# The gate stage of a forgetting attention inside the ramp of its unit loop, and the place of one bit step

## What is computed

```python
q = x @ Wq; k = short_conv(x @ Wk, kconv_w); v = short_conv(x @ Wv, vconv_w)   # 4 taps, silu
q = group_rmsnorm(q, qnw, H); k = group_rmsnorm(k, knw, H)
log_fgate = jax.nn.log_sigmoid(x @ Wf + bf)
cum = jnp.transpose(jnp.cumsum(log_fgate, axis=1), (0, 2, 1))
scores = jnp.einsum('bhtd,bhsd->bhts', qh, kh) * scale + cum[:, :, :, None] - cum[:, :, None, :]
attn = jax.nn.softmax(jnp.where(causal, scores, -jnp.inf), axis=-1)
out = jnp.einsum('bhts,bhsd->bhtd', attn, vh)
out = out / rms(out) * onw * silu(x @ Wg); x = x + out @ Wo
```

## Time and profile before

| | |
|---|---|
| median of 3 runs | 2194.36 us (2193.86 to 2197.66) |
| the profiled execution | 2199.9 us, its span 2198.1 us |
| mean granted TensorE clock | 0.939 |
| PE busy | 1852.4 us (84%) |
| DVE busy | 1541.4 us (70%) |
| ACT busy | 1384.8 us (63%) |
| POOL busy | 1008.2 us (46%) |
| DMA | 84.48 MB, mean 38 GB/s |

### The profile page before, as it was taken

The page is one execution under the profiler, slowest core; times in us unless marked ns, Lnnn a source line. Parts: engine busy times, 40 slices in busy tenths (PEclk is TensorE's granted clock), DMA queues, the critical chain, the costliest instruction groups (busy, mean ns, idle before and its releaser), DMA issues. The chain is left out here.

```text
span 2198.1 us, 36564 instructions
## 1 busy us (share of the span) xinstructions
PE 1852.4 (84%) x12003; PEld 892.8 (41%) x12003; DVE 1541.4 (70%) x2303; ACT 1384.8 (63%) x2346; POOL 1008.2 (46%) x1088
## 2 busy tenths in 40 slices
PE   5558886686976757999999999999999877799996
PEld 2123332542664412555555555555554323222222
DVE  5979996696356957888888888888887637511212
ACT  3547773443344435777777777777776434799995
POOL 0157773363115604676666666666666512400001
PEclk9779998798997978999999999999999979999999
DMA  3000000000000011121211212222122101412110
GB/s 95 0 15 0 0 0 0 1 1 1 0 0 1 1 56 35 48 63 59 61 61 61 60 59 59 59 60 61 61 61 61 41 10 38 120 45 54 49 44 39
DMA packets 71432, 84.48 MB, mean 38 GB/s; under 512 B 20544, under 2 KB 44032, under 8 KB 71168
## 3 DMA queue, kind: packets, MB, share of 16 engines
q1 hardware_dynamic: 69536, 81.69, 12.8%
q10 hardware_dynamic: 1728, 0.67, 0.1%
HBM read 71.95 MB, written 9.57 MB: 37 GB/s over the span
## 5 line engine op out<-in xcount | busy, mean ns | idle before, releaser
L1744 DVE SCALAR_TENSOR_TENSOR fu_kv<-fu_ps_kv,fa_vec,fu_kv 128x511 f32<-128x511 f32 (+2 forms) x384 | 286.3, 746 | 58.9 <-ACT fu_kv L1616 53.7
L2149 ACT ACTIVATE rt_p<-rt_ps_s 128x1024 f32<-128x1024 f32 x256 | 240.3, 1040 | 23.0 <-PE rt_ps_o L2094 17.7
L1827 POOL TENSOR_TENSOR fu_ds<-fu_p 128x768 f32<-128x768 f32 x64 | 115.8, 1809 | 187.8 <-PE fu_ps_ss L1515 185.1
L1475 PE MATMUL fu_ps_s<-fu_qn,fu_kn 64*128 64x512 f32 (+3 forms) x1024 | 190.0, 468 | 1.3 <-ACT fu_p L1675 0.8
L624 POOL TENSOR_TENSOR scan_hC<-scan_h,scan_c 128x1024 f32<-128x1024 f32 x64 | 151.0, 2359 | 71.6 <-DVE scan_h L600 71.6
L1616 ACT ACTIVATE fu_kv<-fu_ps_kv,fa_vec 128x512 f32<-128x512 f32 x128 | 88.3, 690 | 110.6 <-PE fu_ps_kv L1524 67.8
L1505 PE MATMUL fu_ps_n<-fu_p,fu_vt 128*64 128x512 f32 (+3 forms) x1024 | 151.9, 439 | 0.0
L523 PE MATMUL scan_ps_y<-scan_hC,w_ident 128*128 128x512 f32 x256 | 125.7, 614 | 26.4 <-POOL scan_hC L624 14.8
L600 DVE TENSOR_TENSOR_SCAN scan_h<-scan_dA,scan_ps_b 128x1024 f32<-128x1024 f32 x64 | 146.4, 2287 | 2.2
L2094 PE MATMUL rt_ps_o<-rt_p,rt_va 128*32 128x512 f32 x1024 | 137.8, 610 | 10.6 <-ACT rt_p L2149 8.1
L1843 POOL TENSOR_TENSOR fu_kn<-fu_ks,fu_rb 128x512 f32<-128x512 f32 x64 | 81.5, 1273 | 73.4 <-DMA fu_rb<-rms_rows 73.4
(11 more groups left out here) (373 smaller groups left out, 5110.9 us busy)
## 6 DMA issues: line engine op xcount, KB each, us to landing
fu_rb<-rms_rows SPq DMA_DIRECT2D x256, 128.0 KB, 2.9
fu_ro<-rms_rows SPq DMA_DIRECT2D x128, 128.0 KB, 3.0
ra_stackq<-rope_parts SPq DMA_DIRECT2D x168, 32.0 KB
ra_stackk<-rope_parts SPq DMA_DIRECT2D x168, 32.0 KB
w_X<-in_xT SPq DMA_DIRECT2D x4, 512.0 KB, 7.3
fa_wp<-in_wp SPq DMA_DIRECT2D x8, 256.0 KB
fa_cr<-ncum_rows SPq DMA_DIRECT2D x128, 3.0 KB
rope_parts<-ra_hi SPq DMA_DIRECT2D x16, 128.0 KB, 2.7
```

The costliest lines, as they stand in the source:

```text
L1475: pe.matmul(sps[:, h, at:at + T - t * P], k[head(h), t * P:(t + 1) * P], q[head(h), t * P:T], start=(at == 0), stop=False)
L1744: dve.scalar_tensor_tensor(acc, kvps[:, at, 0:T - j], vec[:, a % GA, w:w + 1], acc, ALU.mult, ALU.add).then_inc(done, 1)
L1827: pool.tensor_tensor(DS[:, :, :], P0[p % 2][:, :, P:T], P13[:, :, 0:3 * P], ALU.add).then_inc(s.d1, 1)
L2149: act.activation(pr[k % 2][i][:, :, :], sps[(U * n + u) % RING][:, :, :], ACT.Exp, scale=DH_B ** -0.5).then_inc(s.exp, 1)
```

## The change

The stage forget_gates is removed. Its weight loads go to SP and its memsets to GpSimd in the layernorm "ln5", which now runs inside the function of the attention. Its computation goes into forget_units: the 8 matmuls behind those of unit 1 (into the PSUM tile nps), Abs, Exp and Ln on ScalarE in front of unit 2's tanh, the minimum and the first subtraction on VectorE behind unit 2's keys, the scan with the first split behind unit 3's keys and the rest of the split behind unit 4's. SP stores `ncum_rows` in slot i = -3, loads the broadcasts RB in front of the gate rows CR, and waits for the store before the first CR. ScalarE loads the table of exp and tanh at the start of the block. Scratch is taken from NUM tiles that are not in use yet, and three new tiles. The bit step moves from the end of the odd slot to the next, even slot, behind the cast and the subtraction of the maxima and in front of the taps. Renamed loop variables of TensorE are left out of the diff.

```diff
-def layernorm_stage(nc, name, w, src, dst, loading=False):
+def layernorm_stage(nc, name, w, src, dst, loading=False, held=None):
...
+            if held is not None:
+                @block.sync
+                def _(sp):
+                    sp.dma_start(held.vec[:, :, :], w.vecg_dram.rearrange("g p c -> p g c")).then_inc(held.loaded, 16)
+                    for g in range(GA):
+                        sp.dma_start(held.wp[:, g, :, :], w.wp_dram[g]).then_inc(held.loaded, 16)
+                    sp.dma_start(held.wo[:, :, :], w.woa_dram.rearrange("g p c -> p g c")).then_inc(held.loaded, 16)
+                    sp.wait_ge(held.loaded, 16 * (GA + 2))
+                @block.gpsimd
+                def _(pool):
+                    for k in range(3):
+                        pool.memset(held.cr[k][:, :], 0.0).then_inc(s.zero, 1)
+                    pool.memset(held.mhl[:, :, :, :], 0.0).then_inc(s.zero, 1)
+                    pool.wait_ge(s.zero, 4)
+                    for h in range(2):
+                        for k in range(3):
+                            pool.memset(held.cr[k][64 * h:64 * h + 5, :], 1.0).then_inc(s.made, 1)
+                    pool.wait_ge(s.made, 6)
+                    pool.memset(held.mhl[:, :, :, 0:3], 1.0).then_inc(s.made, 1)
...
-        forget_gates(nc, w, XN, ncum_rows, held)
+        layernorm_stage(nc, "ln5", w, X, XN, held=held)
         forget_units(nc, w, X, XN, ncum_rows, held)
...
# SP of forget_units
-                sp.wait_ge(held.loaded, 16 * (GA + 2))
-                sp.wait_ge(held.stored, 16)
                 for i in range(-AHEAD, U + OUT + 2):
+                    if i == 5 - AHEAD:
+                        sp.wait_ge(s.hi1, 1)
+                        sp.wait_ge(s.mid, 1)
+                        sp.wait_ge(s.lo, 1)
+                        sp.dma_start(ncum_rows, NC[:, :, :]).then_inc(held.stored, 16)
                     u = i + 2
                     if real(u):
                         n, g = divmod(u, GA)
-                        sp.wait_ge(s.sc, seen(u - 2, 3))
-                        for h in range(2):
-                            row = HEADS_A * n + 2 * g + h
-                            sp.dma_start(CR[u % 3][64 * h:64 * h + KF, :], ncum_rows[row, :, :]).then_inc(crs[u % 3], 16)
                         sp.wait_ge(s.put, 16 * (u // WIN + 1))
...
                                 sp.dma_start(RB[head(h), j, :], roots_dram[u // WIN, row:row + 1, :].broadcast_to([64, T])).then_inc(s.rb, 16)
+                        if u == 0:
+                            sp.wait_ge(held.stored, 16)
+                        sp.wait_ge(s.sc, seen(u - 2, 3))
+                        for h in range(2):
+                            row = HEADS_A * n + 2 * g + h
+                            sp.dma_start(CR[u % 3][64 * h:64 * h + KF, :], ncum_rows[row, :, :]).then_inc(crs[u % 3], 16)
...
# TensorE, behind maximum(m, ((0, 0), (2, P)))
+                    if d == 0:
+                        for odd in range(2):
+                            for q in range(B // 2):
+                                f = pe.matmul(nps[32 * q:32 * q + 32, :], w.wf[:, odd, :], XN[:, 2 * q + odd, :], start=(odd == 0), stop=(odd == 1))
+                        f.then_inc(s.f, 1)
...
# ScalarE
+                act.preload_act_table_set("exp_and_others")
                 act.wait_ge(held.loaded, 16 * (GA + 2))
...
+                    if a == 2:
+                        act.wait_ge(s.f, 1)
+                        act.activation(ab[:, :], nps[:, :], ACT.Abs, bias=w.vecs[:, 3:4]).then_inc(s.ab, 1)
+                        act.wait_ge(s.ab, 1)
+                        act.activation(e1[:, :], ab[:, :], ACT.Exp, scale=-1.0).then_inc(s.e, 1)
+                        act.wait_ge(s.e, 1)
+                        act.activation(ln1[:, :], e1[:, :], ACT.Ln, bias=w.one[:, 0:1]).then_inc(s.ln, 1)
                     if real(a):
                         tanh(a, place(a), s.k3, s.thk)
...
# VectorE
                         dve.tensor_tensor(MHL[:, :, :, 4], nm[:, :, :], MHL[:, :, :, 3], ALU.subtract).then_inc(s.ml, 1)
+                    if i % WIN == 0 and windows(i - 2) != (None, None):
+                        begin(i - 1)
                     if real(a):
                         tap(a, 1, 0, place(a), s.tapk, s.k1)
...
                     if real(o):
                         output(o)
+                    if a == 2:
+                        dve.wait_ge(s.ab, 1)
+                        dve.tensor_scalar(mn[:, :], nps[:, :], w.vecs[:, 3:4], 0.0, ALU.add, ALU.min).then_inc(s.mn, 1)
+                        dve.wait_ge(s.mn, 1)
+                        dve.wait_ge(s.ln, 1)
+                        dve.tensor_tensor(ng[:, :], ln1[:, :], mn[:, :], ALU.subtract).then_inc(s.ng, 1)
+                    if a == 3:
+                        dve.wait_ge(s.ng, 1)
+                        dve.wait_ge(s.set, 5)
+                        dve.tensor_tensor_scan(cum[:, :], ones[:, :], ng[:, :], 0.0, ALU.mult, ALU.add).then_inc(s.cum, 1)
+                        dve.wait_ge(s.cum, 1)
+                        dve.tensor_copy(NC[:, 0, :], cum[:, :]).then_inc(s.hi1, 1)
+                        dve.wait_ge(s.hi1, 1)
+                        dve.tensor_tensor(r1[:, :], cum[:, :], NC[:, 0, :], ALU.subtract).then_inc(s.l1, 1)
+                    if a == 4:
+                        dve.wait_ge(s.l1, 1)
+                        dve.tensor_copy(NC[:, 1, :], r1[:, :]).then_inc(s.mid, 1)
+                        dve.wait_ge(s.mid, 1)
+                        dve.tensor_tensor(r2[:, :], r1[:, :], NC[:, 1, :], ALU.subtract).then_inc(s.l2, 1)
+                        dve.wait_ge(s.l2, 1)
+                        dve.tensor_copy(NC[:, 2, :], r2[:, :]).then_inc(s.lo, 1)
...
-                    if q is not None or v is not None:
-                        begin(i)
...
# GpSimd
                 pool.wait_ge(held.loaded, 16 * (GA + 2))
+                pool.memset(ones[:, :], 1.0).then_inc(s.set, 1)
```

More of the change, by code:

```diff
@@ L145, in layernorm_stage @@
         lnv, rstd, step1, step2, fine = ([st.sb(f"{n}{k}", [P, T]) for k in range(2)] for n in ("lnv", "rstd", "v1", "v2", "fine"))
-        s = st.sems("cent kept sq var lnv rstd vr vrr fine wide norm")
+        s = st.sems("cent kept sq var lnv rstd vr vrr fine wide norm zero made")
         with st.block() as block:
@@ L1362, in forget_units @@
         nm = st.sb("nm", [P, NT, 2])
+        ab, e1, ln1, mn, ng, cum = NUM[0:6]
+        r1, r2, ones = (st.sb(n, [P, T]) for n in ("low1", "low2", "ones"))
+        NC = held.nc
         SG = st.sb("sg", [P, T])
@@ L1369, in forget_units @@
         nps, ssps = st.ps("n", [P, T]), st.ps("ss", [P, T])
-        s = st.sems("set kp vp tapk tapv k1 k2 k3 v1 v2 v3 thk thv sk sv vt vc qp qc q2 kk sa so dsq msq mso fold bits ya yb yc yd y1 ye yf yg yh yi r rb ro0 ro1 put "
+        s = st.sems("f ab e ln mn ng cum hi1 l1 mid l2 lo set kp vp tapk tapv k1 k2 k3 v1 v2 v3 thk thv sk sv vt vc qp qc q2 kk sa so dsq msq mso fold bits ya yb yc yd y1 ye yf yg yh yi r rb ro0 ro1 put "
                     "cr0 cr1 cr2 qn kn qm km mx red hi ml rt rr sc ex pv d1 d2 ds n2 nc gp tg sg gated og wo x")
@@ L1536, in _ @@
                         pe.wait_ge(s.ml, b + 1)
-                        for t in range(NT):
-                            k = pe.transpose(mps[:, 1, :].bitcast(BF16)[:, t * P:(t + 1) * P], MHL[:, t, :, :].rearrange("p h c -> p (h c)"), w.identb[:, :])
+                        for j in range(NT):
+                            k = pe.transpose(mps[:, 1, :].bitcast(BF16)[:, j * P:(j + 1) * P], MHL[:, j, :, :].rearrange("p h c -> p (h c)"), w.identb[:, :])
                         k.then_inc(s.rt, 1)
@@ L1550, in _ @@
                         pe.matmul(kvps[:, 1, :], wp[:, g, 2, :], XN[:, n, :], start=True, stop=True).then_inc(s.vp, 1)
-                    if real(f):
-                        pe.wait_ge(s.sv, f + 1)
-                        pe.wait_ge(s.vc, f)
+                    if real(t):
+                        pe.wait_ge(s.sv, t + 1)
+                        pe.wait_ge(s.vc, t)
                         pe.wait_ge(s.nc, seen(p))
-                        for t in range(NT):
-                            k = pe.transpose(nps[:, t * P:(t + 1) * P], VS[f % 2][:, t * P:(t + 1) * P], w.ident[:, :])
+                        for j in range(NT):
+                            k = pe.transpose(nps[:, j * P:(j + 1) * P], VS[t % 2][:, j * P:(j + 1) * P], w.ident[:, :])
                         k.then_inc(s.vt, 1)
@@ L1573, in _ @@
                     if real(p):
-                        pe.wait_ge(s.vc, seen(f + 1))
+                        pe.wait_ge(s.vc, seen(t + 1))
                         pe.wait_ge(s.ex, 3 * p + 3)
@@ L2232, in hybrid_kernel @@
             lambda: None, lambda: ffn0_stages(nc, w, X),
-            lambda: layernorm_stage(nc, "ln5", w, X, XN), lambda: forgetting_attention_stages(nc, w, X, XN),
+            lambda: None, lambda: forgetting_attention_stages(nc, w, X, XN),
```

66 lines of the change are left out of this document (3 added, 63 removed).

## The result

The changed kernel takes 2205.43 us, median of 19 executions (2202.23 to 2211.89); the kernel before took 2199.08 us, median of 19 in the same comparison (2193.86 to 2205.51). The ratio is **1.0028, with a 95% interval of 1.0017 to 1.0038**: slower by 3.7 to 8.4 us. Single executions of one kernel lie up to 12 us apart here, so the traces are compared by stretches. The two profiled executions (2202.23 us, and 2199.9 before) already differ when the changed part begins: the layernorm's first matmul starts at 781.03 us instead of 784.47. They differ again behind it: from the last addition to the end it is 428.0 instead of 430.8 us. What the change does stands between these two points.

The account below looks back on a forecast made before the run. TensorE bounds the unit loop, so other engines matter only through waits holding it up. Terms: -6.3 (gates moved) + 0 + 16.5 - 3.0 - 0.7 = +6.5 us on 2194.36, or 2201 us; own range 2197 to 2206, overall 2186 to 2206.

Parts of the forecast that it names:

- Steady loop: Even slots i = 6 to 54: bit step held by GpSimd's third sum, taps 0.66 us later, 25 times, +16.5 us.
- The precedent of the earlier trace: Late slots before the change: a bit step took 1.49 us instead of 0.19, ending where GpSimd's sum ends.
- Start of the loop: Gate stage in front of the unit loop removed, weight loads hidden under the layernorm: loop starts 12.4 us sooner.
- Ramp: Gate work returning among the first units: slot 2 +3.6 us, slots 3 and 4 +4.1, together +7.7.
- Absorbed at the fold: Ramp, before unit 6's taps: waits for the late fold and a projection shrink, hiding part of the delay, -1.6 us.
- Load order: SP's queue, root broadcasts before gate rows: no effect as TensorE is the bound, 0, between -1 and +1 us.
- End of the loop: Slots 58, 60 and 62: TensorE's wait for the subtraction goes, 3 x 1.0 = -3.0 us.
- First slots: Slot 2: as at the loop's end, with a shorter TensorE wait for the subtraction that goes, -0.7 us.
- not held: Steady loop: the bit step slips in behind the subtraction; -7.2 us in all, 2187 us, faster; chance 0.17.
- half hidden: Steady loop: step held but half hidden, 8.3 instead of 16.5; -1.7 us in all, 2193 us; chance 0.15.
- gates hide wholly: Ramp: moved gates cost nothing, step held as forecast; +0.4 us, 2195 us, chance 0.05; with unheld step 2181, chance 0.03.
- doesn't do what it says: Ramp: gate chain lies wholly on the path, nothing absorbed; 2204.5 us, slower; chance 0.03.

Follow-up runs that it names:

- half sum: The changed kernel with GpSimd's third sum cut to half its columns, leaving out part of the denominators; ratio to the kernel before 0.9990 (0.9973 to 1.0006).
- the step twice: The changed kernel with the bit step issued twice in a row, first into a spare tile; 2217.39 us against 2197.18 in one execution each.
- the gates alone: The changed kernel with only the bit step back at the odd slot's end; ratio to the kernel before 0.9997 (0.9982 to 1.0012), medians 2197.14 against 2199.22 us.
- without the logarithm: Gates moved, bit step at its old place, logarithm replaced by an add of one; layernorm's end to first maximum 52.53 us instead of 55.36.

## Why the prediction was right

Forecast +6.5 us, range -8 to +12; measured +6.35 by the medians and +8.5 between the two traces. In absolute times the forecast was 2201 us, laid on a median of 2194.36 from 3 runs. With the 19 runs of the comparison that median is 2199.08, so the 2205.43 measured lies only just inside the range's end of 2206. The mechanism is the one named; term by term:

- **Steady loop, +16.5: right.** +15.5 in the trace: 0.65 a pair instead of 0.66, in 24 of 25 pairs. In slot 28 the cast reached a gap of GpSimd and the step wasn't held (27.95 us; 27.93 before), and the kernel before had lost 0.15 to 0.2 in each of two others. The precedent of the earlier trace rows, laid on the times of the earlier trace rows, gave the size; the half sum shows that it is the cause. The Trainium skill, "SBUF — State Buffer", section SBUF: two separate sides, has whichever of the two engines starts first hold the shared pair for its whole instruction, where VectorE's has two SBUF inputs or runs in a mode that uses both ports. The trace agrees: 1.16, 0.73, 0.46 and 1.30 us of hold end with the GpSimd operation each time. That the bit step, with its one input, runs in such a mode is not shown otherwise.
- **Start of the loop, -12.4: nearly right.** From the end of the layernorm to the first matmul of the loop 13.20 us became 1.32, so -11.9. The weight loads cost nothing.
- **Ramp, +7.7: its parts.** Slot 2 was +3.6 with the saved table load; the keys of units 0, 2 and 3 lie +2.95 and +1.09 further apart, less 0.67 at the start: +3.4. Slots 3 and 4 were +4.1 and are +4.9, with the two held casts shown in the last section. Absorbed at the fold: -1.6 forecast, -1.3 measured. The ramp's net is -5.0 instead of -6.3, by 0.5 at the start, 0.8 in those slots, 0.3 at the fold, less 0.2 in slot 2 and 0.1 behind it. The drain of 1.38 us per table load that the Trainium skill's "ScalarE: Activation LUTs", section What ACT_TABLE_LOAD costs, adds isn't seen (rows below). By that page the ramp would have been 2.8 us longer, an estimate from its figure (2 x 1.38).
- **Load order, 0: right** (1.0006, pairs unchanged).
- **End of the loop, -3.0: the step that failed.** The stretch 56 to 63 gained 0.9 us. The step said that the wait of 1.03 us for the subtraction goes once the cast reaches the gap. In slot 58 of the kernel after:

```profile
1669.06 0.18 DVE L1725 CAST fa_mhl<-fu_nm 128x8 bf16<-128x8 f32 x1
1669.28 1.30 DVE L1727 TENSOR_TENSOR fa_mhl<-fu_nm,fa_mhl 128x8 bf16<-128x8 f32 x1
...
1669.27 1.26 POOL L1827 TENSOR_TENSOR fu_ds<-fu_ds,fu_p 128x512 f32<-128x512 f32 x1
...
1670.63 0.40 PE L1499 MATMUL fu_ps_m<-w_identb,fa_mhl 128*128 128x128 bf16 x4 [0.81 <-DVE fa_mhl L1727]
```

The cast was free, the subtraction behind it was held by the sum that began 0.01 us before it, and TensorE still waited 0.81 us. Slot 60 shows the same 0.81; in slot 62 the subtraction passed and the wait is gone, and slot 61 has a new one of 0.81 instead of 0.45. I followed one of two chained operations through the gap and forgot the second.

- **First slots, -0.7: near by luck.** They gained 1.1 us, but not where the forecast had it. In slot 2 the subtraction is held for 1.31 us too, and TensorE's wait there only fell from 0.66 to 0.44. The gain of 0.85 lies in slot 3 (12.58 us instead of 13.43), at whose end the step at its old place waited 0.91 us for the fold. That a step at the old place can hold up the slot while it waits for its fold was in no term.

The ramp (+1.3) and the end of the loop (+2.1) were taken too well, the steady loop (-1.0) and the first slots (-0.4) too badly, so the traces say +8.5 where the sum says +6.5. The medians' interval, +3.7 to +8.4, holds the one and ends at the other; that +6.35 lies so near +6.5 is luck. Of the rivals, "not held" and "half hidden" fall by the pairs, "gates hide wholly" by the ramp, and "doesn't do what it says" by the 1.3 us absorbed. Not priced at all was the old place's own risk, the late fold: it doesn't show in the profiled execution of the kernel before, it does once the gates are moved, and at the old place it costs 1.2 to 1.35 us in the pair and some 0.25 in the next one.

## What to carry to other kernels

A short SBUF operation of VectorE costs what GpSimd is doing at that moment: place it by GpSimd's gaps, and look at how far the gap's edges are from its time of issue, at the old place as well as the new. Where there is a choice, put it behind the last operation that the bound engine waits for; two taps and a gate product further on, a loss of 0.3% had become a gain of 0.4%. Each of two chained short operations needs its own gap.

## What the hardware showed that was not expected

- **Who gets in first is a toss of 0.01 us,** as far as the profile can tell. In the kernel with the step twice the same pair of times gives 0.18 or 1.07 us; the winner makes the other wait (GpSimd's square 1.09 instead of 1.04 us).
- **Casts of 512 columns are held too.** In the ramp of the kernel after, beside GpSimd's square of keys and small root operations:

```profile
824.63 1.21 DVE L1766 TENSOR_TENSOR_SCAN fu_num<-fu_ones,fu_num 128x512 f32<-128x512 f32 x1
825.88 1.08 DVE L1768 CAST fa_nc<-fu_num 128x512 bf16<-128x512 f32 x1
...
831.28 0.42 DVE L1773 CAST fa_nc<-fu_low 128x512 bf16<-128x512 f32 x1
...
832.46 1.42 DVE L1777 CAST fa_nc<-fu_low 128x512 bf16<-128x512 f32 x1
...
824.80 1.88 POOL L1834 TENSOR_TENSOR fu_sqk<-fu_ks 128x512 f32<-128x512 f32 x1 [4.21 <-DVE fu_ks L1754]
...
832.57 1.03 POOL L1834 TENSOR_TENSOR fu_sqk<-fu_ks 128x512 f32<-128x512 f32 x1
```

  0.42 us is the free one; the two held ones end 0.28 us behind the square beside them. The hold goes both ways: the first square takes 1.88 us instead of 1.04. What held it is the scan that began 0.17 us before it and ended at 825.84; from there to the square's end it is 0.84 us.
- **Table loads without a drain.** ScalarE between two passes:

```profile
814.16 0.63 ACT L1640 ACTIVATE fu_num<-fu_num 128x512 f32<-128x512 f32 x1
814.82 1.28 ACT L1642 ACT_TABLE_LOAD   x1
816.11 0.72 ACT L1642 ACTIVATE fu_num<-fu_num,w_consts 128x512 f32<-128x512 f32 x1
816.85 1.28 ACT L1587 ACT_TABLE_LOAD   x1
818.14 0.60 ACT L1587 ACTIVATE fu_ps_kv<-fu_kv 128x512 f32<-128x512 f32 x1
```

- **Late folds.** With the gates alone, in all three disturbed places (the folds of slots 6, 24 and 44), a fetch of instructions over DMA falls between the fold's issue and the slot's first maximum; in slots 18 and 52 one does as well, and the fold is on time (in slot 28 it is 0.03 us late). It isn't this kernel's alone. In all eleven traces of kernels with the gates moved, the changed kernel's among them, SP takes 3.2 us to issue the folds of slots 6 and 44. It takes 2.9 in the other steady slots, and in all of them in the three kernels with the gates at their old place. By the semaphore events the fold of slot 24 lands 1.5 to 1.8 us behind the end of its issue in ten of the eleven, with a fetch that begins 0.4 us behind that end. In the eleventh, without the logarithm, and in those three kernels no fetch begins there, and it lands after 1.15 us. So the gates' move brings the late folds, the old place of the step makes a loss of them, and the new places don't. That the shifted code, by where its fetches fall, is the cause fits most of this, but no run tested it.
